# Attention on one core: one PSUM bank for the accumulator, seven for score tiles, relu per bank, sums in two bursts a round

## The reference

```
q, k, v = split(layernorm(x) @ W_attn + b_attn)          # 16 heads of 8
s = q @ k.T;  s = s - s.mean(-1);  mad = abs(s).mean(-1) + 1e-6
s = where(causal, s / mad * score_gain, -1000)
r = maximum(s, 0) ** 4
att = r / (r.sum(-1) + 1e-6);  y = att @ v;  x = x + y @ W_proj + b_proj
```

## Time and profile before

| | |
|---|---|
| median of three runs | 506.7 us |
| span of the profiled execution | 505.4 us |
| attention, eight quads | about 121.6 to 406.5 us, 35.6 us a quad |
| PE, DVE, ACT, POOL busy over the span | 441.9, 402.7, 342.0, 243.8 us |

### The profile page before, as it was taken

The page is one execution under the profiler, slowest core; times in us unless marked ns, Lnnn a source line. Parts: engine busy times, 40 slices in busy tenths (PEclk is TensorE's granted clock), DMA queues, the critical chain, the costliest instruction groups (busy, mean ns, idle before and its releaser), DMA issues. The chain is left out here.

```text
span 505.4 us, 8943 instructions
## 1 busy us (share of the span) xinstructions
PE 441.9 (87%) x2736; PEld 168.3 (33%) x2736; DVE 402.7 (80%) x832; ACT 342.0 (68%) x576; POOL 243.8 (48%) x180
## 2 busy tenths in 40 slices
PE   0879999664799999999999999999999995879996
PEld 0323444431232332333333322323323354334442
DVE  5884556976898998999989899989988969784443
ACT  3413223554999999999999999999989931523221
POOL 5940000333777686776877677676876720000000
PEclk9979999975999999999999999999999998799999
DMA  4300000025714205105114124043002300000001
GB/s 118 75 1 0 1 0 0 6 65 127 208 33 78 60 1 95 43 1 93 42 30 71 34 51 84 0 72 63 0 0 50 85 12 0 1 1 0 21 21 42
DMA packets 17796, 21.32 MB, mean 42 GB/s; under 512 B 4748, under 2 KB 10476, under 8 KB 17772
## 3 DMA queue, kind: packets, MB, share of 16 engines
q1 hardware_dynamic: 17452, 20.95, 19.2%
q10 hardware_dynamic: 320, 0.07, 0.1%
HBM read 13.02 MB, written 7.86 MB: 41 GB/s over the span
## 5 line engine op out<-in xcount | busy, mean ns | idle before, releaser
L1206 POOL TENSOR_TENSOR arena<-arena 128x1024 f32<-128x1024 f32 (+1 forms) x120 | 204.0, 1722 | 63.7 <-ACT arena L1178 63.5
L1136 DVE SCALAR_TENSOR_TENSOR arena<-bank,masks 128x1024 f32<-128x1024 f32 (+1 forms) x160 | 174.9, 1114 | 28.9 <-PE bank L1048 28.6
L1178 ACT ACTIVATE arena<-arena 128x1024 f32<-128x1024 f32 (+1 forms) x160 | 148.5, 961 | 8.8 <-DVE arena L1136 5.8
L1048 PE MATMUL bank<-Q,K 128*128 128x512 bf16 (+3 forms) x384 | 91.4, 334 | 10.6 <-DMA K<-k_parts 9.2
L1048 PE MATMUL bank<-K,Q 128*128 128x512 bf16 (+3 forms) x384 | 90.4, 331 | 11.6 <-DVE arena L1136 11.5
L1144 DVE TENSOR_SCALAR_CACHE_REDUCE bank<-bank 128x128 f32<-128x128 f32 (+7 forms) x128 | 94.8, 772 | 0.0
L1168 ACT ACTIVATE bank<-bank 128x128 f32<-128x128 f32 (+7 forms) x128 | 80.9, 632 | 8.9 <-PE bank L1048 8.6
L1079 PE MATMUL bank<-arena,Vq 128*32 128x512 f32 (+3 forms) x768 | 79.6, 495 | 0.0
L588 ACT ACTIVATE arena<-bank 128x512 f32<-128x512 f32 x40 | 23.9, 597 | 76.5 <-PE bank L463 76.5
L689 DVE TENSOR_TENSOR arena<-arena,bank 128x512 f32<-128x512 f32 x40 | 27.4, 686 | 42.8 <-PE bank L467 42.7
L1079 PE MATMUL bank<-arena,ones_rows 128*32 128x512 f32 (+3 forms) x640 | 61.1, 473 | 0.0
(11 more groups left out here) (122 smaller groups left out, 355.4 us busy)
## 6 DMA issues: line engine op xcount, KB each, us to landing
Q<-q_parts SPq DMA_DIRECT2D x24, 192.0 KB
att<-arena SPq DMA_DIRECT2D x28, 128.0 KB, 2.0
K<-k_parts SPq DMA_DIRECT2D x16, 128.0 KB
K<-k_parts SPq DMA_DIRECT2D x8, 192.0 KB
X<-in_L_attn_x SPq DMA_DIRECT2D x4, 256.0 KB, 4.6
K<-k_parts SPq DMA_DIRECT2D x16, 64.0 KB
out_x<-X SPq DMA_DIRECT2D x4, 256.0 KB, 2.3
q_parts<-arena SPq DMA_DIRECT2D x3, 256.0 KB
```

The source lines that it names most:

```text
L1048: last = nc.tensor.matmul(bank[:, lo + shift:hi + shift], left[par][:, g, blk * P:(blk + 1) * P], right[par][:, g, s0:s0 + hi - lo], start ...
L1136: nc.vector.scalar_tensor_tensor(Y(r, g)[:, lo - off(r):hi - off(r)], tiles[slot["lower", r, g]][:, lo:hi], 0.0, mask, ALU.max, ALU.mult). ...
L1178: nc.scalar.activation(z, Y(r, g)[:, tile_low(r) - off(r):T - off(r)], ACT.Square)\
L1206: nc.gpsimd.tensor_tensor(z, z, z, ALU.mult).then_inc(fourth_p, 1)
```

## The change

The accumulator becomes one bank (number 7). Queries 0 to 511 go to rows 0 to 15 of each head's 32 partitions (numerator in 0 to 7, denominator in 8, relu sums in 9), queries 512 to 1023 to rows 16 to 31, on the same 512 columns: the weights are 48 columns wide in SBUF and a window of 32 is taken from them, shifted by 16 for the second half. The other seven banks hold single-bank units of the score tiles; a list written out by hand (`TILE_BANKS`) gives each unit's bank. PE waits for each bank by itself, DVE does the relu of a lower tile bank by bank, an upper tile of two banks (side by side) is still summed as before. Each round's sums are added after steps 1 and 3 only. POOL takes the fourth power of all tiles but those of g = 3 in rounds 1 and 3. The stored sums are 32 x 512 a head, and what reads them follows.

```diff
 def square_by_gpsimd(r, g):
-    return g < 3
+    return not (g == G - 1 and r in (1, 3))
+TILE_BANKS = [0, 1, 2, 4, 0, 5, 1, 2, 3, 5, 6, 0,
+              2, 3, 4, 6, 0, 1, 3, 4, 5, 0, 1, 2,
+              4, 5, 0, 2, 6, 3, 0, 5, 1, 6, 0, 3,
+              2, 1, 5, 0, 4, 2, 5, 6, 0, 2, 3, 4,
+              6, 0, 1, 2, 3, 4, 5, 6]
+ACC_BANK = 7
+HALF_ROWS = 16
+def half_weights(w, half):
+    return w[:, HALF_ROWS * (1 - half):HALF_ROWS * (1 - half) + 32]
+def tile_units():
+    banks = iter(TILE_BANKS)
+    units = []
+    for r in range(NR):
+        for g in range(G):
+            if r == NR - 1:
+                units += [("lower", r, g, 1, next(banks)), ("upper", r, g, 1, next(banks))]
+            else:
+                units += [("lower", r, g, half, next(banks)) for half in (0, 1)]
+                first = next(banks)
+                units += [("upper", r, g, half, first + half) for half in (0, 1)]
+    return units
...
-        m.ones_rows = sb("ones_rows", [P, 32])
+        m.ones_rows = sb("ones_rows", [P, 48])
-        m.Vq = sb("Vq", [P, NB, G, 32])
+        m.Vq = sb("Vq", [P, NB, G, 48])
-        att_dram = nc.dram_tensor("att", [B * N_HEAD, 4, D, T], F32, kind="Internal").ap()
+        att_dram = nc.dram_tensor("att", [B * N_HEAD, 32, SPAN], F32, kind="Internal").ap()
...
-    sums = a.take(T)
-    tiles = m.psum[0:3]
-    acc = m.psum[3]
+    sums = a.take(SPAN)
+    acc = m.bank[:, ACC_BANK * SPAN:(ACC_BANK + 1) * SPAN]
...
+            def wait_bank(q, kind, r, g, half):
+                bank = bank_of[kind, r, g, half]
+                n = units.index((kind, r, g, half, bank))
+                back = next(k for k in range(1, 2 * len(units)) if units[n - k][4] == bank)
...
             def fill(q, par, r, g, kind):
                 left, right = (K, Q) if kind == "lower" else (Q, K)
+                for half in halves(r):
+                    wait_bank(q, kind, r, g, half)
...
+                    if kind == "lower":
+                        last.then_inc(lower_ready, 1)
+                if kind == "upper":
+                    last.then_inc(upper_ready, 1)
...
-                start = what == "relu" and r == 0
-                stop = what == "power" and (r == NR - 1 or (r == NR - 2 and s0 < SPAN))
+                half = s0 // SPAN
+                at = s0 - half * SPAN
+                start = first and what == "relu" and r == 0
+                stop = last and what == "power" and r == NR - 1
                 for g in range(G):
                     src = (Z if what == "power" else Y)(r, g)[:, lo - off(r):hi - off(r)]
-                    w = Vq[:, blk, g, :] if what == "power" else m.ones_rows[:, :]
-                    mm = nc.tensor.matmul(acc[32 * g:32 * (g + 1), s0:s0 + hi - lo], w, src, start=start,
+                    w = half_weights(Vq[:, blk, g, :] if what == "power" else m.ones_rows[:, :], half)
+                    mm = nc.tensor.matmul(acc[32 * g:32 * (g + 1), at:at + hi - lo], w, src, start=start,
                                           stop=stop, skip_group_check=True)
...
-                return [work[g * len(work) // G:(g + 1) * len(work) // G] for g in range(G)]
+                return [[], work[:len(work) // 2], [], work[len(work) // 2:]]
...
-                    nc.vector.scalar_tensor_tensor(Y(r, g)[:, lo - off(r):hi - off(r)],
-                                                   tiles[slot["lower", r, g]][:, lo:hi], 0.0, mask,
-                                                   ALU.max, ALU.mult).then_inc(relu_done, 1)
+                    for half in halves(r):
+                        dve.wait_ge(lower_ready, q * NRELU + relus_upto(r, g, half))
+                        at = bank_of["lower", r, g, half] * SPAN
+                        y0 = half * SPAN - off(r)
+                        mask = masks[:, 0, 0:SPAN] if r == NR - 1 else masks[:, r, half * SPAN:(half + 1) * SPAN]
+                        nc.vector.scalar_tensor_tensor(Y(r, g)[:, y0:y0 + SPAN], m.bank[:, at:at + SPAN], 0.0, mask,
+                                                       ALU.max, ALU.mult).then_inc(relu_done, 1)
...
-                nc.scalar.activation(sums, acc[:, :], ACT.Copy).then_inc(sums_out, 1)
+                nc.scalar.activation(sums, acc, ACT.Copy).then_inc(sums_out, 1)
...
-        self.num_dmas = [1, 1 + G]
+        self.num_dmas = [2, 2 + 2 * G]
...
-            engine.dma_start(self.num[at:at + D, b * T:], sums[32 * g:32 * g + D, :]).then_inc(self.num_loaded[b], 16)
+            for half in range(2):
+                row = 32 * g + HALF_ROWS * half
+                engine.dma_start(self.num[at:at + D, b * T + half * SPAN:b * T + (half + 1) * SPAN], sums[row:row + D, :])\
+                    .then_inc(self.num_loaded[b], 16)
```

More of the change, by code:

```diff
@@ L289, in attention_constants @@
                                        channel_multiplier=1)
[L291 to L293 removed]
+    for half in range(2):
+        nc.gpsimd.affine_select(out=m.pick[:, half], in_=m.pick[:, half], compare_op=ALU.not_equal, fill=1.0,
+                                base=32 * (HEAD_ROW[B - 1] + N_HEAD - G) - HALF_ROWS * half - D,
+                                pattern=[[-1, 2], [-32, HB]], channel_multiplier=1)
     for r in range(NR - 1):
@@ L968, in attention, with upper_at @@
     NV, NA, NP4, NA4 = all_of(by_v), all_of(by_a), all_of(sq_p), all_of(sq_a)
[L971 to L978, removed]
+    units = tile_units()
+    bank_of = {unit[:4]: unit[4] for unit in units}
+    halves = lambda r: (1,) if r == NR - 1 else (0, 1)
+    NRELU = sum(len(halves(r)) for r, g in steps)
+    relus_upto = lambda r, g, half: sum(len(halves(rr)) for rr, gg in steps[:steps.index((r, g))]) + 1 + halves(r).index(half)
+    def upper_at(r, g, col):
+        half = halves(r)[0]
+        return bank_of["upper", r, g, half] * SPAN + col - half * SPAN
     def quads(engine, body):
@@ L1022, in _ @@
         def _(pe):
[L1023 to L1027, removed]
-                    return
[L1029 to L1038, removed]
+            def wait_bank(q, kind, r, g, half):
+                bank = bank_of[kind, r, g, half]
+                n = units.index((kind, r, g, half, bank))
+                back = next(k for k in range(1, 2 * len(units)) if units[n - k][4] == bank)
+                if n < back and first_quad(q):
+                    return
+                k, rr, gg, hh, _ = units[n - back]
+                qq = q - 1 if n < back else q
+                if k == "lower":
+                    pe.wait_ge(relu_done, qq * NRELU + relus_upto(rr, gg, hh))
+                elif by_v(rr, gg):
+                    pe.wait_ge(upper_v, qq * NV + count(by_v, (rr, gg)))
+                else:
+                    pe.wait_ge(upper_a, qq * NA + count(by_a, (rr, gg)))
@@ L1040, in fill @@
             def fill(q, par, r, g, kind):
                 left, right = (K, Q) if kind == "lower" else (Q, K)
[L1043 to L1049, removed]
@@ L1050, in fill @@
-                last.then_inc(lower_ready if kind == "lower" else upper_ready, 1)
+                for half in halves(r):
+                    wait_bank(q, kind, r, g, half)
+                    at = bank_of[kind, r, g, half] * SPAN - half * SPAN
+                    for blk, col, seq in tile_blocks(r):
+                        for lo, hi in bank_pieces(col, col + width(blk)):
+                            if lo // SPAN == half:
+                                s0 = seq + lo - col
+                                last = nc.tensor.matmul(m.bank[:, at + lo:at + hi], left[par][:, g, blk * P:(blk + 1) * P],
+                                                        right[par][:, g, s0:s0 + hi - lo], start=True, stop=True)
+                    if kind == "lower":
+                        last.then_inc(lower_ready, 1)
@@ L1107, in _ @@
             quads(pe, body)
-            pe.wait_ge(relu_done, NQUAD * STEPS)
+            pe.wait_ge(relu_done, NQUAD * NRELU)
             pe.wait_ge(upper_v, NQUAD * NV)
@@ L1164, in body @@
                         act.wait_ge(upper_ready, n)
-                        shift = -SPAN if r == NR - 1 else 0
                         for blk, col, seq in tile_blocks(r):
-                            src = tiles[slot["upper", r, g]][:, col + shift:col + width(blk) + shift]
+                            src = m.bank[:, upper_at(r, g, col):upper_at(r, g, col) + width(blk)]
                             last = nc.scalar.activation(src, src, ACT.Relu,
@@ L1276, in tensor @@
                     for k, into in ((0, self.den_ps), (1, self.upper_ps[B - 1])):
-                        last = nc.tensor.matmul(into[n * HB:(n + 1) * HB, :], m.pick[:, k, :],
-                                                sums[:, n * QT:(n + 1) * QT], start=(k == 0), stop=True,
+                        half, at = n * QT // SPAN, n * QT % SPAN
+                        last = nc.tensor.matmul(into[n * HB:(n + 1) * HB, :], m.pick[:, half, k, :],
```

(1 more changed line is left out.)

39 lines of the change are left out of this document (18 added, 21 removed).

## The result

The changed kernel takes 487.7 us (median of 4, 487.4 to 489.2) against 506.8 for the kernel before: ratio 0.9636, 95% interval 0.9614 to 0.9658, 19 us less. The forecast was 492.8, range 486 to 502. The span of the profiled execution is 485.7 us (505.4 before).

A forecast was written before the change was run, and what follows sets the result against it. A ring of PE, DVE and ACT, ACT first, bounds the 35.6 us quad. Afterwards 33.1 (DVE) + 0.3 + 0.3 + 0.1 = 33.8; seven quads give 12.6, the first 1.3, together 13.9 us: 492.8, range 486 to 502.

The forecast's parts named there:

- the forecast's own mechanism: Attention: DVE becomes first engine, plus small burst and ACT losses; period 33.3 to 34.4 us, 489 to 498, 60 in 100.
- the free ring: Rival: with seven banks neither bursts nor ACT's lag are felt; period DVE's 32.9 to 33.1 us, 486, 10 in 100.
- the 0.4 for ACT and for latencies: Per quad: 0.3 us added for ACT's work in rounds 1 and 3, and 0.1 for semaphore latencies.
- The ring: PE fills score tiles, DVE and ACT empty them, PE gets them back; 1.1 us a quad lost above ACT.
- ACT's share: ACT is first in the kernel before, with 34.5 us of own work a quad, falling to 31.2 afterwards.
- the whole part on the fourth powers: Three of ACT's five fourth powers per quad go to POOL: ACT 2.9 us less, POOL 4.8 more, at 30.6.
- the signs that I gave: Expected in the new profile: period near 33.8, ACT idle before its squares, POOL at 30.6 us, ten bursts.
- DVE's term: Relu in halves adds 0.07 us per tile, 1.1 a quad; DVE's own work goes from 32.0 to 33.1.
- dear halves: Rival: each half relu also costs its recorded overlap, 0.16 us per tile; period 34.9 us, 501, 16 in 100.
- The long burst: Round 0's burst of 2.38 us is the only one over PE's lead, by 0.2 to 0.3 us.
- PE's edges: Seven fewer bursts of sums between fills, 0.21 us each: PE's own work 1.5 us a quad less, at 32.2.
- Starvation: Rival: DVE runs dry at long bursts as PE gets its last bank late; up to 531 us, 9 in 100.

The follow-up runs named there:

- a_pool: The kernel before with POOL taking 18 instead of 15 of the 20 fourth powers: 506.8 us, ratio 0.9991, 35.60 us a quad.
- b_pool_old: The changed kernel with POOL back at 15 of 20 fourth powers: 487.8 us, ratio 0.9639 to the kernel before, 33.23 us a quad.
- b_spread: The changed kernel with the sums spread over the four steps as before: 493.1 us, ratio 0.9735 to the kernel before, 33.97 us a quad.
- d_late_release: The changed kernel with PE waiting for both half relus before refilling either bank of a lower tile: 505.5 us, ratio 0.9983 to the kernel before.
- b_one_burst: The changed kernel with one burst of sums a round, after step 3 (round 1 unchanged): 518.2 us, ratio 1.0250 to the kernel before.
- a_bursts: The kernel before with only the sums changed, to two bursts a round: 518.1 us, ratio 1.0234, 37.10 us a quad.
- c_best: The changed kernel with bursts evened, one upper sum moved from DVE to ACT and one fourth power from POOL to ACT: 485.1 us, ratio 0.9573.

## Why the prediction was right, and where it was not

487.7 us lies inside the stated range of 486 to 502, but outside the 489 to 498 that I gave the forecast's own mechanism; its period, 33.21, is just below that mechanism's 33.3 to 34.4. The range holds it because it takes in the free ring. Its terms add up to 0.6 us a quad too much: DVE's own work was 0.5 too high and the 0.4 for ACT and for latencies was not there, against a stop 0.3 dearer than given. That it came this close is in part luck: it had the wrong first engine in the kernel before, and was spared only because its figure for the kernel after was built on DVE.

**The ring.** That three engines wait on each other through the score tiles, and that seven banks released singly end it, was right, and it was more than the forecast made of it. I took the ring's loss as 1.1 us above ACT. It was 35.6 less DVE's own work of 31.6, 4.0 us, and all but 0.6 of that went; 1.1 came back as the cost of the halves.

**ACT's share failed.** "So ACT is first" was wrong, and with it the whole part on the fourth powers as a term of the sum: a_pool and b_pool_old show it at 0.00 and 0.02 us of the 2.39. The own work of 34.5 us was too high by 0.9 or more: subtracting listed waits leaves every gap too short for the list in the own work. Of the signs that I gave, one failed with it: ACT's idle time in the changed kernel is not before its squares and released by DVE, but before its upper sums and released by PE, 2.5 us in four places. The better reading stood in the earlier trace rows: the waits that come in pairs, DVE for PE and PE for DVE, close a loop; nothing there waited long for ACT. I named the loop and then went by the busiest engine.

**DVE's term.** Halves at + 0.07 each, 1.1 us a quad, held (0.60 us from start to start). The own work before was mis-sized in the same way as ACT's: 32.0 for about 31.6 (32.6 less the halves' 1.1, to 0.1), so that 33.1 became 32.6. The rule of the Trainium skill, "Perfetto Trace Analysis", "Optimizing Scalar/DVE Operations", would have put DVE, by an estimate from its 125 ns, 2.0 us above the kernel before: at 34.0, or 33.6 from the own work of 31.6. Both are above the measured quad of 33.21, stop included; the trace decides against the 125 ns here. The rival of dear halves fell with it.

**The long burst.** Right in place and number of stops: one, after round 0's second burst. 0.58 us for the forecast 0.2 to 0.3. The 0.3 for ACT and 0.1 for latencies were not there. 32.6 + 0.6 = 33.2: the outcome is near that of the free ring in time (32.9 to 33.1), not in mechanism.

**PE's edges.** 1.5 us less work was the forecast. PE's periods less its listed waits, 33.8 us in b_spread and 32.5 in the changed kernel, put it at some 1.3, an estimate from two upper bounds. It was worth 0.76 on the path, and less than nothing without the seventh bank.

**Starvation** was a real neighbour. d_late_release delays the release by one half relu, 0.6 us, and the kernel is back at 0.998 of before; I had put break-even at 0.8 us. By the rival's own rule a delay of 0.6 costs some 1.4 us a quad more than no delay; it cost 2.3, while in b_one_burst the rule asked for a third too much. With a_bursts it shows that the burst plan alone has the sign of that rival.

**POOL.** 30.4 us as forecast, and the power sums of the steady quads were never late: no matmul waits for POOL. The waits view puts 0.4 us ahead of one weight load (216.74) down to it, but by POOL's rows, at 1.86 us a tile, that tile was ready near 213.0 us. At 20 of 20 it falls behind.

**The first quad and the end.** The first quad was given 1.3 us and gave 2.9: DVE's first relu starts at 120.65 us, before at 121.64, and the stretch from it to the second quad's first relu falls from 35.05 to 33.19. That start is the relu per bank: PE's first fill begins at 120.56 us before and 120.41 after, and the relu follows it by 1.08 us where it waits for two banks, by 0.24 where it waits for one. The end moved by 0.1 us (99.1 us from DVE's last upper sum to the end before, 99.2 after). One effect there I had not foreseen; it is told below.

## What to carry to other kernels

Where engines pass buffers round a ring, ask first which pair of waits closes a loop and how long each buffer is held, not which engine is busiest: taking 2.3 us of work from a 96% busy engine gave nothing, while giving back each bank one half relu earlier was worth 2.3 us a quad. Batching work on the producer pays only as long as the consumers' buffers outlast the batch, so the two are changed together, and a buffer count is tested with the batch that it will meet. Own work is best sized from a run in which the engine has no waits; the period less the listed waits is too high.

## What the runs showed of the hardware

Some DVE instructions on SBUF alone are held up while POOL works. In the changed kernel POOL's last fourth powers run from 385.24 to 389.32 us, beside DVE's work on the denominators:

```profile
385.24 4.08 POOL L1245 TENSOR_TENSOR arena<-arena 128x512 f32<-128x512 f32 x4 [0.67 <-ACT arena L1217]
...
387.98 0.44 DVE L1361 TENSOR_SCALAR low<-low,slope 128x256 f32<-128x256 f32 x1
388.45 1.14 DVE L1362 TENSOR_TENSOR low<-low 128x256 f32<-128x256 f32 x1
...
389.63 0.42 DVE L1363 TENSOR_TENSOR low<-low 128x256 f32<-128x256 f32 x1
```

The first multiply takes 1.14 us and ends just after POOL does, the same one after it 0.42. With all 20 on POOL, which then works to 396.59 us, the same stretch has 1.14 to 1.15 us three times (the third at 394.54) and a scalar operation of 0.35 us at 2.00:

```profile
390.15 2.00 DVE L1361 TENSOR_SCALAR low<-low,slope 128x256 f32<-128x256 f32 x1
...
392.18 1.14 DVE L1362 TENSOR_TENSOR low<-low 128x256 f32<-128x256 f32 x1
...
393.36 1.15 DVE L1363 TENSOR_TENSOR low<-low 128x256 f32<-128x256 f32 x1
```

In c_best, where POOL is done by 384.98, L1361 takes 0.35 and L1362 0.42 us. The relus, with one operand in PSUM and one in SBUF, keep 0.60 us whatever POOL does. Not every instruction on SBUF is held: the reciprocal that starts at 395.72 us beside POOL keeps its 1.75 us, and L1361 above takes only 0.44. The Trainium skill has this on its page "SBUF — State Buffer", section "SBUF: two separate sides": one port pair is shared, as an exclusive lock for a whole instruction, between GpSimd and those VectorE instructions that have two SBUF inputs (against a GpSimd instruction that reads SBUF, as POOL's multiplies do) or run in a two-port mode. The trace agrees, with 0.7 us for a multiply of two SBUF inputs and 1.65 for the scalar operation; that the latter ran in a two-port mode, no view shows.
